# Seven block products in place of eight in the first expert layer

## What is computed

```python
logits = jnp.einsum('bld,ed->ble', x, gate_weight)
kth_val = jnp.sort(logits.reshape(-1))[expert_k - 1]
gates = logits * (logits >= kth_val)
h = jax.nn.gelu(jnp.einsum('bld,ehd->bleh', x, w1) + b1, approximate=True)
y = jnp.einsum('bleh,edh->blde', h, w2) + b2.T[None, None]
out = jnp.einsum('blde,ble->bld', y, gates)
```

## Time and profile before

| | us |
|---|---|
| median of three runs | 2075.0 (2073.8 to 2075.75) |
| the profiled execution | 2074.38 |
| its span in the trace | 2072.6 |
| PE matmul busy | 1978.3 (95%) |
| DVE busy | 1271.3 (61%) |
| ACT busy | 725.1 (35%) |
| POOL busy | 102.0 (5%) |
| DMA | 102.47 MB, mean 49 GB/s |

### The profile page before, as it was taken

One profiled execution on the slowest core, in us unless ns is written; L12 is line 12 of the kernel. 1 busy time (PEld: TensorE's weight loads), 2 busy tenths in 40 slices (PEclk: granted clock), 3 DMA queues, 4 the chain that ended last, 5 costly groups with the idle time before them and its releaser, 6 DMA issues.

```text
span 2072.6 us, 29677 instructions
## 1 busy us (share of the span) xinstructions
PE 1978.3 (95%) x9252; PEld 1426.3 (69%) x9252; DVE 1271.3 (61%) x2415; ACT 725.1 (35%) x1206; POOL 102.0 (5%) x294
## 2 busy tenths in 40 slices
PE   7899999999958999999999999999999999999998
PEld 5734333333337877888888888888888888888887
DVE  5588888888626675555565465456456546555544
ACT  4447666666722222222222222222222222222222
POOL 4201001110111000000000000000000000000000
PEclk9979999999969999999999999999999999999999
DMA  7832222222110010000010010001010001000100
GB/s 242 328 105 78 78 79 69 80 69 69 38 42 21 0 64 32 31 10 15 26 35 16 31 30 15 10 26 40 11 31 31 15 10 48 18 10 10 46 30 36
DMA packets 76457, 102.47 MB, mean 49 GB/s; under 512 B 29026, under 2 KB 47204, under 8 KB 74340
## 3 DMA queue, kind: packets, MB, share of 16 engines
q1 hardware_dynamic: 76388, 101.67, 15.7%
HBM read 75.81 MB, written 25.56 MB: 49 GB/s over the span
## 4 chain that ended last, share of the span: by engine, by line
PE 69%; DVE 1%; ACT 0%; issue 0%; DVEq 0%; ACTq 0%
PE ps_h L1878 35%; PE ps_y L1892 35%; DVE h_lo L2099 0%; DVE h_hi L2095 0%; ACT gelu L1998 0%; DVE gated L2164 0%; ACT L1998 0%; DVE out_T_acc L2169 0%; DVE w_lo L2040 0%; DVE w_lo L2207 0%; DVE w_hi L2038 0%; PE ps_h L1960 0%; PE ps_h L1928 0%; DVEq L2233 0%; DVEq L2094 0%
## 5 line engine op out<-in xcount | busy, mean ns | idle before, releaser
L1998 ACT ACTIVATE gelu<-ps_h,b 128x512 f32<-128x512 f32 x512 | 352.7, 689 | 1084.1 <-PE ps_h L1878 1018.3
L2095 DVE CAST h_hi<-gelu 128x512 fp32r<-128x512 f32 x512 | 219.7, 429 | 575.6 <-ACT gelu L1998 570.1
L1878 PE MATMUL ps_h<-x_hi,w_hi 128*128 (+1 forms) x1024 | 409.2, 400 | 10.1 <-DVE w_lo L2040 8.8
L1892 PE MATMUL ps_y<-h_hi,w_hi 128*128 128x512 f32 x1024 | 405.1, 396 | 6.1 <-DVE h_lo L2099 6.1
L1878 PE MATMUL ps_h<-x_lo,w_hi 128*128 (+1 forms) x1024 | 406.0, 396 | 0.0
L1878 PE MATMUL ps_h<-x_hi,w_lo 128*128 (+1 forms) x1024 | 405.7, 396 | 0.0
L1892 PE MATMUL ps_y<-h_lo,w_hi 128*128 128x512 f32 x1024 | 404.9, 395 | 0.0
L1892 PE MATMUL ps_y<-h_hi,w_lo 128*128 128x512 f32 x1024 | 404.8, 395 | 0.0
L2099 DVE TENSOR_TENSOR h_lo<-gelu,h_hi 128x512 fp32r<-128x512 f32 x512 | 357.3, 698 | 16.5
L957 DVE TENSOR_REDUCE low<-ps_s 128x1 f32<-128x512 f32 x512 | 321.8, 682 | 41.2 <-PE ps_s L814 39.1
L1071 ACT ACTIVATE probs_T<-ps_t 128x512 f32<-128x512 f32 x384 | 207.5, 599 | 106.9 <-PE ps_t L824 104.8
(11 more groups left out here) (210 smaller groups left out, 1218.3 us busy)
## 6 DMA issues: line engine op xcount, KB each, us to landing
gate<-gates_scratch SPq DMA_DIRECT2D x64, 256.0 KB, 3.1
q_st<-q_scratch SPq DMA_DIRECT2D x192, 64.0 KB, 2.2
k_st<-k_scratch SPq DMA_DIRECT2D x192, 64.0 KB, 2.3
k_scratch<-k_hl SPq DMA_DIRECT2D x8, 1024.0 KB, 3.9
q_scratch<-q_hl SPq DMA_DIRECT2D x8, 1024.0 KB, 5.1
w_raw<-in_w1T SPq DMA_DIRECT2D x8, 1024.0 KB, 5.1
w_raw<-in_w2T SPq DMA_DIRECT2D x7, 1024.0 KB, 5.3
v_scratch<-v_out SPq DMA_DIRECT2D x8, 544.0 KB, 5.2
```

The source lines that it names most:

```text
L1878: mm = pe.matmul(ps_h[:, j % RING, :], w[:, k, at], x[:, k, bass.ds(c * SEQ, SEQ)], start=(i == 0), stop=(i == len(parts) - 1))
L1892: mm = pe.matmul(ps_y[s][:, d, :], w[:, j, at], h[:, j % RING, :], start=(j == 0 and i == 0), stop=(j == HT - 1 and i == 2))
L1998: act.activation(gelu[:, j % GELUS, :], ps_h[:, j % RING, :], ACT.Gelu_apprx_tanh, bias=b1[p][:, j:j + 1]).then_inc(gelu_done, 1)
L2095: dve.tensor_copy(h_hi[:, j % RING, :], gelu[:, j % GELUS, :]).then_inc(h_hi_done, 1)
```

## The change

Expert 1 stays as it is. For experts 2 to 8 the first layer is done by twins of two chunks. W1 is taken as 2 by 2 blocks (hidden half by feature half), the twin's tokens as 2 by 2 blocks (feature half by chunk). Strassen's scheme in the form with fifteen sums makes their product from seven block products in place of eight.

- Four sums of token blocks (T1 to T4) per twin are the same for all experts. POOL makes them during the search, ten operations of 128x512 a twin (`block_sums`). ACT makes their high parts (`split_block`, behind gelu tiles 7 to 10, 14 to 17, 21 to 24 and 27 to 30), DVE the low parts (`block_low`, behind search rounds 8 to 11, 15 to 18, 22 to 25, 28 to 31). SP stores all seven blocks of a twin to DRAM (`store_blocks`). From expert 2 on SP loads a twin's blocks (3584 KB) over the tokens, into one half of `x_hi` and `x_lo`, while the other half is in use (`load_set`).
- Four sums of weight blocks (S1 to S4) are made per expert by DVE (`set_sums`), their high parts by ACT (`split_set`), their low parts by DVE (`set_lows`). The high parts of W2 move from DVE to ACT (`split_w2`).
- A group is one quarter of the hidden half by a twin: four cells (2 tiles by 2 chunks), seven products of three matmuls. Banks of `ps_h` gather sums over several products: x takes products 0, 2, 4 and 5, v takes 1 and 6, z takes 3. ACT copies x out three times on its way (`copied`), DVE adds such a copy to z or v for three of the cells (`add_corner`); the fourth is x at the end. Gelu, halves and second layer follow for each cell. PE puts the second layer's cells of the group before between the products.
- Some semaphores that counted similar things are merged into one.

```diff
+SPLIT_AT = (8, 15, 22, 28)
...
+                sp.wait_ge(w_ready, 2 + (twin + 1) * CELLS)
...
+                    x = (x_hi, x_lo)[part]
+                    to = scratch["blocks"][twin, part]
+                    first = twin * 2 * SEQ
+                    for dst, src in ((to[:, 0, 0:SEQ], x[:, 0, first:first + SEQ]),
+                                     (to[:, 1, 0:2 * SEQ], x[:, 1, first:first + 2 * SEQ]),
+                                     (to[:, 0, SEQ:4 * SEQ], staged[:, 0:3, :].rearrange("p b t -> p (b t)")),
+                                     (to[:, 1, 2 * SEQ:3 * SEQ], staged[:, 3, :])):
+                        sp.dma_start(dst, src.bitcast(F32)).then_inc(t_stored, 16)
...
+                number = (e - 1) * TWINS + twin
+                if isinstance(e, int) and e == 1 and twin == 0:
+                    sp.wait_ge(h_in_psum, TWINS * HT)
+                else:
+                    sp.wait_ge(h_in_psum, BATCH * HT + (number - 1) * QUADS * BLOCKS)
+                for part, x in enumerate((x_hi, x_lo)):
...
+            sp.wait_ge(w_ready, 2)
+            load_w2(1)
+            for twin in range(TWINS):
+                store_blocks(twin)
+            sp.wait_ge(t_stored, 8 * 16 * TWINS)
+            load_set(1, 0, 0)
             sp.wait_ge(gates_T_ready, 1)
...
+            def block_sums(twin):
+
+                c1, c2 = (slice(c * SEQ, (c + 1) * SEQ) for c in (2 * twin, 2 * twin + 1))
+                b11, b12, b21, b22 = ([x[:, k, c].bitcast(F32) for x in (x_hi, x_lo)] for k in range(KT) for c in (c1, c2))
...
+                pool.tensor_tensor(t1, b12[0], b11[0], ALU.subtract).then_inc(t_summed, 1)
+                pool.tensor_tensor(t3, b22[0], b12[0], ALU.subtract).then_inc(t_summed, 1)
+                pool.wait_ge(t_summed, done + 1)
+                pool.tensor_tensor(t1, t1, b12[1], ALU.add).then_inc(t_summed, 1)
...
+                pool.wait_ge(t_summed, done + 8)
+                pool.tensor_tensor(t4, b21[0], t2, ALU.subtract).then_inc(t_summed, 1)
+                pool.wait_ge(t_summed, done + 9)
+                pool.tensor_tensor(t4, t4, b21[1], ALU.add).then_inc(t_summed, 1)
+
+            pool.wait_ge(h_ready, RING)
+            for twin in range(TWINS):
+                block_sums(twin)
...
+            def product(e, twin, i, kind, a, b, start):
+
+                bank = bank_of(kind, i)
+                pair, at = divmod(i, 2)
+                w = [w1_pairs[pair][:, at, part, a, :] for part in range(2)]
+                x = [x_block(twin, b, part) for part in range(2)]
+                for n, (wp, xp) in enumerate(((0, 0), (0, 1), (1, 0))):
+                    mm = pe.matmul(bank, w[wp], x[xp], start=start and n == 0, stop=n == 2, skip_group_check=not start)
+                mm.then_inc(h_in_psum, 1)
...
+            def group_starts(e, twin, i, k):
+
+                n = group_of(e, twin, i)
+                first = isinstance(e, int) and e == 1 and twin == 0
+                if k == 0:
+                    if i == 0:
+                        number = (e - 1) * (TWINS // 2) + twin // 2
+                        pe.wait_ge(set_loaded[twin % 2], number * 64 + 64)
+                    if twin == 0 and i in (0, 2):
+                        pe.wait_ge(w_ready, weight_no(e, 3 if i == 0 else 5))
+                    pe.wait_ge(gelu_done, BATCH * HT - 3 + RING if first and i == 0 else cell_no(n, 0) - 1 + RING)
+                    product(e, twin, i, "x", A11, B11, True)
+                else:
+                    if first and i < 2:
+                        pe.wait_ge(gelu_done, BATCH * HT - 2 + 2 * i + RING)
+                    else:
+                        pe.wait_ge(corner_done, 3 * n - 3)
+                    product(e, twin, i, "v", S1, T1, True)
+
+            def group_goes_on(e, twin, i, cell):
+
+                n = group_of(e, twin, i)
+                pe.wait_ge(copied, 3 * n + 1)
+                product(e, twin, i, "x", S2, T2, False)
+                if isinstance(e, int) and e == 1 and twin == 0 and i == 0:
+                    pe.wait_ge(gelu_done, BATCH * HT - 1 + RING)
+                else:
+                    pe.wait_ge(corner_done, 3 * n - 2)
+                product(e, twin, i, "z", A12, B21, True)
+                cell(1)
+                pe.wait_ge(copied, 3 * n + 2)
+                product(e, twin, i, "x", S3, T3, False)
+                cell(2)
+                pe.wait_ge(copied, 3 * n + 3)
+                product(e, twin, i, "x", A22, T4, False)
+                cell(3)
+                pe.wait_ge(corner_done, 3 * n + 2)
+                product(e, twin, i, "v", S4, B22, False)
...
+            def second_cell(e, p, twin, i, c):
+
+                n = group_of(e, twin, i)
+                s = (0, 1, 0, 1)[c]
+                j = i + (0, QUADS, QUADS, 0)[c]
+                if i == 0 and c < 2:
+                    pe.wait_ge(y_taken, chunk_no(e, 2 * twin + s) + 1)
+                pe.wait_ge(h_ready, cell_no(n, c) + 1 + RING)
+                for d in range(KT):
+                    at = slice(d * P, (d + 1) * P)
+                    for m, (w, h) in enumerate(((w2_hi[p], h_hi), (w2_hi[p], h_lo), (w2_lo[p], h_hi))):
+                        mm = pe.matmul(ps_y[s][:, d, :], w[:, j, at], h[:, c, :],
+                                       start=(i == 0 and c < 2 and m == 0), stop=(i == QUADS - 1 and c >= 2 and m == 2))
+                mm.then_inc(w2_done, 1)
+
+            def group(e, twin, i, cell):
+                for k in range(2):
+                    group_starts(e, twin, i, k)
+                cell(0)
+                group_goes_on(e, twin, i, cell)
...
+            def split_block(at):
+
+                twin, b = divmod(at, CELLS)
+                if b == 0:
+                    act.wait_ge(t_summed, (twin + 1) * SUM_STEPS)
+                    wait(act, t_stored, twin * 8 * 16)
+                act.activation(t_hi[:, b, :], t_sum[:, b, :], ACT.Copy).then_inc(w_hi_done, 1)
+
...
+            def split_set(e, pair):
+
+                if isinstance(e, int) and e == 1:
+                    act.wait_ge(t_stored, 8 * 16 * TWINS)
+                    if pair == 1:
+                        act.wait_ge(h_in_psum, BATCH * HT)
+                else:
+                    act.wait_ge(h_in_psum, product_no(group_of(e - 1, TWINS - 1, 2 * pair + 1), BLOCKS - 1))
+                act.wait_ge(w_ready, weight_no(e, 2 + 2 * pair))
+                for hi, lo, raw in set_parts(pair):
+                    ins = act.activation(hi, raw, ACT.Copy)
...
                 for j in range(HT):
                     gelu_tile(0, 0, c, j)
+                    for twin, start in enumerate(SPLIT_AT):
+                        if start - 1 <= c * HT + j < start - 1 + CELLS:
+                            split_block(twin * CELLS + c * HT + j - start + 1)
...
+            def group(e, p, twin, i, before):
+
+                n = group_of(e, twin, i)
+                x = ps_h[:, 0, :]
+                act.wait_ge(h_in_psum, product_no(n, 0))
+                act.activation(copies[1][:], x, ACT.Copy).then_inc(copied, 1)
+                before()
+                act.wait_ge(h_in_psum, product_no(n, 2))
+                act.activation(copies[0][:], x, ACT.Copy).then_inc(copied, 1)
+                take_corner(e, p, twin, i, 0)
+                act.wait_ge(h_in_psum, product_no(n, 4))
+                act.activation(copies[1][:], x, ACT.Copy).then_inc(copied, 1)
+                take_corner(e, p, twin, i, 1)
+                act.wait_ge(h_in_psum, product_no(n, 5))
+                gelu_cell(e, p, n, i, 2, x)
...
+            def block_low(at):
+
+                twin, b = divmod(at, CELLS)
+                dve.wait_ge(w_hi_done, 2 + at + 1)
+                dve.tensor_tensor(t_lo[:, b, :], t_sum[:, b, :], t_hi[:, b, :].bitcast(F32), ALU.subtract).then_inc(w_ready, 1)
+
+            for i in range(1, BITS + 1):
                 search_round(i, i % RING)
+                for twin, start in enumerate(SPLIT_AT):
+                    if start <= i < start + CELLS:
+                        block_low(twin * CELLS + i - start)
...
+            def set_sums(e, pair):
+
+                a11, a12, a21, a22 = raw_blocks(pair)
+                if pair == 0:
+                    dve.wait_ge(raw_loaded[0], e * 16 + 16)
+                dve.tensor_tensor(s_sum[:, 0, :], a21, a22, ALU.add)
+                dve.tensor_tensor(s_sum[:, 2, :], a11, a21, ALU.subtract).then_inc(set_step, 1)
+                dve.wait_ge(set_step, set_no(e, pair) + 1)
+                dve.tensor_tensor(s_sum[:, 1, :], s_sum[:, 0, :], a11, ALU.subtract).then_inc(set_step, 1)
+                dve.wait_ge(set_step, set_no(e, pair) + 2)
+                dve.tensor_tensor(s_sum[:, 3, :], a12, s_sum[:, 1, :], ALU.subtract).then_inc(w_ready, 1)
+
+            def set_lows(e, pair):
+                dve.wait_ge(w_hi_done, hi_no(e, W2_PIECES + pair + 1))
+                for hi, lo, raw in set_parts(pair):
```

(64 more changed lines are left out.)

353 lines of the change are left out of this document (223 added, 130 removed).

## The result

| | before | after |
|---|---|---|
| median (range, runs) | 2075.15 us (2073.8 to 2075.75, 4) | 2144.7 us (2143.5 to 2147.8, 4) |
| the profiled execution | 2074.38 | 2144.74 |
| its span | 2072.6 | 2142.9 |
| PE matmuls | 9252 | 8916 |
| DVE busy | 1271.3 (61%) | 1515.1 (71%) |

The median moved by 69.6 us. The ratio is 1.0338, 95% interval 1.032 to 1.0356: 3.4% slower, with 336 matmuls fewer. 2131 us had been forecast.

A forecast was written before the change was run, and what follows sets the result against it. The expert stage was taken as bound by the number of matmuls, 0.233 us each. From 2074.4 us, -78.4 + 63 + 7 + 51 + 14 = +56.6 gave 2131 us, range 2084 to 2165 (80 in 100).

The forecast's parts named there:

- 336 matmuls less: Expert stage, first layer: 21 matmuls per group instead of 24, at 0.2333 us each, 78.4 us saved.
- bank of the odd chunk: Group 1 of each twin: PE waits for DVE to release a PSUM bank, 1.9 or 3.3 us, 63 together.
- start and end of the scheme: Expert 2's group 0 without second-layer cells, 3 us, and cell 3 4 us late at the very end: 7 together.
- search: Threshold search: POOL's four bursts of block sums cost 51 us through waits, port lock and lower clock; bounds 34 and 60.
- gates: After the search: gates' store and loads queue behind block stores and perhaps the set load; 14 us, bounds 5 and 30.
- twin 0's burst: Search, first burst: time enough for its sums, but the port lock holds seven operations or so, 7 us.
- the waits of the three others: Search, bursts for twins 1 to 3: ACT waits for all ten sums, costing 11.6, 11.6 and 13.5 us.
- the low clock behind them: Search: after standing, PE runs about a dozen matmuls at 0.42 us, 2.4 us for each of three bursts.
- the lock between DVE and POOL: Search: shared ports make DVE operations wait for POOL; 33 or 36 us for all bursts if the lock were all.
- the gain stays: Rival, 13 in 100: DVE's chain doesn't reach the bank's release, twins cost at most 18 us; 2045 us.
- late set loads: Rival, 7 in 100: each twin starts waiting for x blocks; 5 us at each of 28 twins, 2270 us.
- The ordinary groups: Expert stage: everything in time in an ordinary group; a rival had PE wait 0.3 us in each of 112, 2165 us.

The follow-up runs named there:

- the profiled execution without the waits: Kernel after the change, with the odd chunk's gating ahead of split 3 and the second weight set's low halves behind the next corner: 2078.51 us, ratio 1.0028.
- the kernel with everything reordered: Changed kernel with odd chunk, low halves, gates, later splits and last split all reordered, bursts at tiles 7, 14, 21, 28: 2044.51 us, ratio 0.9864.
- later splits: Changed kernel with ACT's block copies two gelu tiles later (behind tiles 9, 16, 23, 29): 2137.01 us, ratio 1.0309.
- The last two kernels: Changed kernel with all re-orderings, 2044.51 us; the same with two blocks split per round and bursts at rounds 5, 12, 19, 26, 2029.7 us.
- the gates first: Changed kernel with the last store of blocks and the first set load put behind the sixth gate load: 2131.7 us, ratio 1.0283.

## Why the prediction was right

Direction and size were right: two losses, each of the order of the gain, were found where the forecast had put them. That the sum came within 14 us owes something to luck, since a search 8 us too long stood against a clock loss of 16 us that no term had. Step by step, in the account of the profiled span, which grew by 70.3 us:

| step | forecast | measured |
|---|---|---|
| 336 matmuls less | -78.4 | 9252 to 8916, still 0.233 apart |
| bank of the odd chunk | +63 | +55.3 idle, and 6.2 of another stall in its place in two twins |
| clock in the expert stage | none | +15.8 |
| start and end of the scheme | +7 | +5.9 (1.9 and 3.9) |
| search | +51 | +43.4 |
| gates | +14 | +14.2, and 2.4 of low clock behind it |
| twins 0.2 us longer | none | about +6 |

- **The bank wait** was laid out from durations of the kernel before: 1.9 per twin and 3.3 in an expert's first. Measured: 1.92, and 3.08 to 3.16. The forecast's 9.1 per expert was right to a few tenths; over all, 55.3 instead of 63, since the very first twin has 2.42 and two first twins of an expert had another stall of 3.23 and 2.98 in its place. What it missed is the price behind such a wait. The earlier trace rows shows a clock that falls after 6 us of idle time; that it also falls after 1.9 was charged to no term. The nine dipped twins have 15.8 us more PE busy time than at 42.2 us each. Seven of them, with 11.9 of the 15.8, have only the bank wait; the other two have the other stall. In the profiled execution without the waits all of it is gone, while PE's own order stayed, so the link is shown for that one execution.
- **The search** came out 8 us under its term. Its parts: twin 0's burst 2.3 (forecast 7); the waits of the three others 9.8, 9.8 and 13.5 over a normal round (11.6, 11.6, 13.5); the low clock behind them 2.5, 1.5 and 2.2 (2.4 each); the rest small. Two steps were mis-sized. In the three others the 1.4 us of DVE operations was not there: the gelu behind twin 1's burst was done 14.7 us after the burst's start (670.03 to 684.71), not 16.4. And there is the lock between DVE and POOL, 7 us taken from the earlier trace rows, where both DVE operations waited for POOL. In the search most of it falls into the wait of 1.02. The 1.29 us for an operation of 512 columns, interpolated from the earlier trace rows, was measured as 1.26 to 1.8 (below). The step also left out that ACT waits for the stores in the same place. That changed no number here, as the stores were 3 us shorter than the burst, but someone who had acted on it by shortening the burst would have got less than half of the gain hoped for.
- **The gates** were right, but with a wide bound. The order on SP and what lands behind what had been read correctly: first the stores (768.17 to 780.24), then the load, then the gates.
- **What no step named.** 180 matmuls at 0.2333 are 42.0 us, and with the wait of 1.92 an ordinary twin would take 43.92; it takes 44.12, so 0.2 more, 5.6 us over 28 twins. Besides, PE stood for 3.23 and 2.98 us with "issue" as the reason, that is, for nothing that the profile shows. These 6.2 us replaced two bank waits of about 3.1, so they hardly changed this sum, but they stayed (2.9 and 2.7) when the bank waits went:

```profile
1239.35 0.79 PE L2053 MATMUL ps_h<-x_hi,w_pair 128*128 128x512 f32 x1 [3.23 <-issue]
...
1597.10 0.79 PE L2053 MATMUL ps_h<-x_hi,w_pair 128*128 128x512 f32 x1 [2.98 <-issue]
```

They lie 357.75 us apart, two experts, and each stands at the first matmul of group 1 in an expert's first twin. That is where PE's loop over pairs of experts (`pe.Fori(0, PAIRS - 1)`) begins its second and its third turn. Its body is now 1440 matmuls written out. In the kernel before, the loop has three turns as well, but with short loops inside, and no such stall. So the jump back is the likely cause; no run changed the loop, and it is not shown.
- **The rivals.** That the gain stays was wrong in the forecast's terms, but the experiments show how near it was: the kernel with everything reordered does the same arithmetic. The late set loads did not appear: the largest load lands after 10.2 us (page's median), a twin lasts 44. The ordinary groups do not wait.

## What to carry to other kernels

When a change makes one engine's work smaller and another's order new, list for each wait what stands ahead of the releasing operation on its engine although the waiting one does not need it; here two DVE operations moved ahead of one split were worth 59 us of 2144. A wait in a long dense stage of matmuls can cost more than its length, for the clock may fall behind it, and a gain made elsewhere can be lost there. And where a step waits for two things that start at the same moment, shortening the longer one gains only up to the other; give both a distance.

## What the runs showed of the hardware

- **The clock falls behind short waits, and not always.** Behind waits of 1.92 to 3.2 us of PE, matmuls went at 0.43 us, the lower level, in nine twins of 26 of the kernel after, in twelve with later splits and in none with the odd chunk and the low halves moved. The last two kernels have no bank wait over 0.5 us either, yet one twin of 26 and three of 26 have a lowered clock: three of these four hold a stall of 2.6 to 3.2 us at the loop's turn, and in the fourth PE had just waited 1.13, 0.41 and 0.22 us. In the kernel without a lowered clock such stalls (2.90 and 2.71 us) left it at 1.00. Which of the twins it hits differed from kernel to kernel with the same waits. What decides is open.
- **DVE and POOL take turns.** In the kernel after, POOL's sums and DVE's operations beside them:

```profile
670.03 1.29 POOL L1940 TENSOR_TENSOR t_sum<-x_hi 128x512 f32<-128x512 f32 x1 [26.63 <-DVE t_lo L2425]
671.28 1.48 POOL L1941 TENSOR_TENSOR t_sum<-x_hi 128x512 f32<-128x512 f32 x1
672.72 1.79 POOL L1943 TENSOR_TENSOR t_sum<-t_sum,x_lo 128x512 f32<-128x512 f32 x1
...
682.21 1.26 POOL L1957 TENSOR_TENSOR t_sum<-t_sum,x_lo 128x512 f32<-128x512 f32 x1
```

```profile
671.52 1.25 DVE L2417 SCALAR_TENSOR_TENSOR candidate<-change,next_bit,candidate 128x1 int32<-128x1 int32 x1
672.70 0.68 DVE L2378 TENSOR_TENSOR h_lo<-gelu,h_hi 128x512 fp32r<-128x512 f32 x1
673.30 0.47 DVE L2407 TENSOR_SCALAR_CACHE_REDUCE gate<-gate,candidate 128x256 f32<-128x256 f32 x1
```

The operation on one column, else 0.21 us, waits until POOL's ends (671.28 + 1.48 = 672.76). The low half behind it runs at its full speed of 0.68, and POOL's sum is stretched to 1.79 instead. The count with its accumulator takes 0.47 as ever. So in these rows DVE loses what remains of one POOL operation in a round, about 1 us, not the time of all its own. The Trainium skill (SBUF — State Buffer, Who interferes with whom) says that the two hold a port pair under an exclusive lock for a whole instruction and that a tensor_scalar which also writes its accumulator does not take it; both agree with these rows.

- **A small store behind a large load lands late.** The gates' stores, issued at 782.25 right behind the load of a set, let the first gate's load start only at 792.20. With the gates first they took 3.1 us (769.60 to 772.74). Whether they stand in line behind the load or share something with it, no run separates.
